# Two transformer-like layers on one core: where VectorE takes the last table doublings, the factor sums, unit 0's sum and batch 2's moments

## What is computed

```python
x = _layernorm(x + _L0_attn_ref(x, t))       # irfft(rfft(x) * rfft(t)), the first 1024 rows
x = _layernorm(x + _L0_ffn_ref(x, ...))      # shared expert + top 2 of 8 experts
x = _layernorm(x + _L1_attn_ref(x, phazor, phazor_init, last_conv_re, last_conv_im))
x = _layernorm(x + _L1_ffn_ref(x, ...))      # shared expert + top 2 of 8 experts

def _L1_attn_ref(...):
    ph = ph / mag * jnp.exp(-mag)            # one complex number per channel
    prog = ph[None, :] ** t                  # t = 0 .. 1023
    filt = prog * ph_init[None, :]
    conv = jnp.fft.ifft(filt_fft * x_fft, axis=1)[:, :L, :]
    return (conv + last_conv * prog * ph).real
```

## Time and profile before

| | us |
|---|---|
| median of 3 runs | 315.94 (315.78 to 316.88) |
| the profiled execution, whole | 315.59 |
| its span, first to last instruction | 313.8 |
| PE busy | 275.5 (88%) |
| DVE busy | 238.9 (76%) |
| ACT busy | 153.8 (49%) |
| POOL busy | 130.1 (41%) |
| mean granted TensorE clock | 0.962 of full |

### The profile page before, as it was taken

The page is one execution under the profiler, slowest core; times in us unless marked ns, Lnnn a source line. Parts: engine busy times, 40 slices in busy tenths (PEclk is TensorE's granted clock), DMA queues, the critical chain, the costliest instruction groups (busy, mean ns, idle before and its releaser), DMA issues.

```text
span 313.8 us, 3733 instructions
## 1 busy us (share of the span) xinstructions
PE 275.5 (88%) x994; PEld 157.0 (50%) x994; DVE 238.9 (76%) x563; ACT 153.8 (49%) x521; POOL 130.1 (41%) x203
## 2 busy tenths in 40 slices
PE   8699903878988599969999999999999989999993
PEld 7598803546643235425554454545445444444472
DVE  2898799795999966989698779868896863874710
ACT  0318464347722168744656467457637551632323
POOL 3668608814000122148766744874675210110112
PEclk9899985899999789999999999999999999999999
DMA  6992000008556000191009204800860293097111
GB/s 195 332 350 70 0 0 0 0 7 323 243 240 267 0 2 2 58 424 58 0 24 427 91 1 176 362 0 5 323 249 1 96 397 115 4 373 230 34 36 33
DMA packets 19269, 43.54 MB, mean 139 GB/s; under 512 B 1968, under 2 KB 14256, under 8 KB 15024
## 3 DMA queue, kind: packets, MB, share of 16 engines
q1 hardware_dynamic: 16240, 41.56, 35.5%
q10 hardware_dynamic: 2880, 1.74, 1.9%
q0 software_dynamic: 128, 0.00, 0.0%
HBM read 40.94 MB, written 2.36 MB: 138 GB/s over the span
## 4 chain that ended last, share of the span: by engine, by line
issue 30%; PE 22%; POOL 20%; DVE 19%; ACT 4%; DMA 3%; SPq 1%; POOLq 0%; ACTq 0%; DVEq 0%
PE ps L416 8%; PE ps L516 5%; DVE third L1318 4%; POOL rs L972 3%; DMA third<-in_fwd 3%; POOL second L1013 2%; POOL second L1008 2%; POOL second L1001 2%; POOL second L1009 2%; POOL rs L991 2%; POOL second L1002 2%; ACT tok L676 2%; PE ps L434 2%; POOL ve L987 1%; PE ps L513 1%
## 5 line engine op out<-in xcount | busy, mean ns | idle before, releaser
L516 PE MATMUL ps<-third,w_out 128*128 128x512 f32 x240 | 109.8, 601 | 0.0
L1318 DVE TENSOR_TENSOR third<-ps,first 128x512 f32<-128x512 f32 x120 | 73.4, 680 | 0.3
L516 PEld LDWEIGHTS ps<-third,w_out 128*128 128x128 f32 x240 | 45.0, 194 | 52.3 <-issue 44.7
L699 ACT ACTIVATE first<-ps 128x512 f32<-128x512 f32 x32 | 19.1, 597 | 22.9 <-PE ps L497 14.7
L968 POOL TENSOR_TENSOR ve<-ssq,eps 128x4 f32<-128x4 f32 x15 | 3.0, 199 | 65.4 <-ACT xy L736 51.3
L961 POOL TENSOR_TENSOR rs_<-ve_,half_neg 128x8 f32<-128x8 f32 x4 | 6.6, 1658 | 56.3 <-DVE ve_ L1236 56.3
L416 PE MATMUL ps<-second,third 128*128 128x256 f32 x96 | 24.3, 404 | 0.7 <-DVE second L1137 0.7
L1327 DVE TENSOR_TENSOR second<-ps,xT 128x512 f32<-128x512 f32 x15 | 10.2, 681 | 15.7 <-PE ps L516 15.7
L1353 DVE TENSOR_TENSOR_SCAN second<-col,second 128x512 f32<-128x512 f32 x16 | 20.8, 1337 | 1.5 <-POOL second L1001 1.5
L416 PEld LDWEIGHTS ps<-second,third 128*128 128x128 f32 x96 | 18.9, 203 | 5.7 <-issue 3.3
L1307 DVE TENSOR_TENSOR first<-ps,first 128x512 f32<-128x512 f32 x16 | 11.0, 686 | 12.8 <-PE ps L491 8.8
(11 more groups left out here) (288 smaller groups left out, 532.9 us busy)
## 6 DMA issues: line engine op xcount, KB each, us to landing
first<-gates SPq DMA_DIRECT2D x32, 1024.0 KB, 6.8
out<-xy SPq DMA_DIRECT2D x7, 256.0 KB, 4.8
third<-in_inv SPq DMA_DIRECT2D x1, 1536.0 KB, 12.6
xy<-in_L_attn_x SPq DMA_DIRECT2D x8, 128.0 KB, 8.3
xy<-in_L_attn_x ACTq DMA_DIRECT2D x8, 128.0 KB, 8.3
third<-in_fwd SPq DMA_DIRECT2D x2, 512.0 KB, 9.3
w_out<-in_L_ffn_w SPq DMA_DIRECT2D x2, 512.0 KB
third<-in_fwd ACTq DMA_DIRECT2D x1, 512.0 KB, 5.3
```

Source lines behind the costliest of these rows:

```text
L516: last_ = mm(y_ps[:], w_out[l][:, 1 + e], hs[(EXPERTS * n + e) % 16], start=False, stop=(e == EXPERTS - 1))
L699: run(sil[kind], gate_ps[:], ACT.Silu).then_inc(silu_done, 1)
L1318: tt(hs[(EXPERTS * n + e) % 16], rows[:], wbc[n % 2][:, e], MUL).then_inc(scaled, 1)
```

## The change

Four moves, and no operation is added or taken away:

- `inverse_transform(1, ...)` is cut behind its ninth late operation, and `add_input(0)` is put in the cut. It stood at the head of VectorE's slot 1.
- `moments1(2)` stood behind it, ahead of both `hidden` of slot 1, and stands behind them now.
- `table_sums(8)` and `table_sums(9)`, which stood around the late inverse sums, stand behind rows 0 and 4 of `scale_rows(2)`. ScalarE's `table_products(9)` goes from ahead of slot 0 into slot 1, behind `squares(0)`.
- `factor_sums` goes from slot 2 (behind unit 3's rows, ahead of the first scan) to slot 1 (behind unit 2's rows). ScalarE's `factor_products` goes from the end of its slot 1 to ahead of `copy_channels(1, 4)`.

```diff
@@ ScalarE, slot(n)
                 if n:
                     squares(n - 1)
+                if n == 1:
+                    table_products(9)
                 if n in TURN_SLOT:
                     normalise1(TURN_SLOT[n][0])
                 if n:
                     normalise(n - 1)
                 if n - 1 in ROUTE_SLOT:
                     copy_gates(ROUTE_SLOT[n - 1])
+                if n == 1:
+                    factor_products()
                 if n in TURN_SLOT:
                     copy_channels(1, TURN_SLOT[n][0])
                     normalise1(TURN_SLOT[n][1])
@@
                 if 0 <= n - 3 < GROUPS:
                     normalise3(n - 3)
-                if n == 1:
-                    factor_products()
@@ ScalarE, ahead of the slots
             table_products(8)
-            table_products(9)
@@ VectorE, inverse_transform, part 1
                     stt(f, p, -0.5, e, MUL, ADD).then_inc(step, 1)
+                if part == 2:
                     own("y3")
@@ VectorE, slot(n)
-                if n:
+                if n > 1:
                     add_input(n - 1)
-                if n in (1, 2):
-                    moments1(n + 1)
+                if n == 2:
+                    moments1(3)
@@
                 between = {}
+                if n == 1:
+                    moments1(2)
+                    between[0] = lambda: table_sums(8)
+                    between[4] = lambda: table_sums(9)
@@
                     scale_rows(n + 1, between)
-                if n == 2:
+                if n == 1:
                     factor_sums()
@@ VectorE, ahead of the slots
             inverse_transform(0, 1)
+            inverse_transform(0, 2)
             moments1(0)
@@
             scale_rows(1, {})
-            table_sums(8)
             inverse_transform(1, 1)
-            table_sums(9)
+            add_input(0)
+            inverse_transform(1, 2)
```

## The result

The changed kernel takes 312.81 us in the median of 4 runs (312.33 to 313.10), the kernel before 315.86 (315.10 to 316.88) on the same chip: ratio 0.9897, 95% interval 0.9869 to 0.9925. That is 3.1 us faster; 3.7 were forecast (312.2, range 311.6 to 314.4). The profiled execution is 312.82 us long, its span 311.0. Each set has its own runs of the kernel before.

A forecast was written before the change was run, and what follows sets the result against it. TensorE was taken as the bound from slot 3 on. 0.53 + 3.17 + 0.2 = 3.9 us, less 0.2 for the clock, gave 3.7: 315.59 to 311.9 profiled, median 0.35 above, 312.2 us, range 311.6 to 314.4.

The forecast's parts named there:

- What bounds the kernel: From the 18th slice (133 us), slot 3 on, TensorE is the bound, at 9 tenths in nearly every slice.
- the sum 4.8 us sooner: Slot 1: unit 0's sum starts 4.80 us sooner, but TensorE then idles 4.8 us ahead of unit 4's transposes; worth nothing itself.
- The chain through batch 2: Slot 1, batch 2's moments to unit 5's normalisation: unit 5's rows and the rest of TensorE's slot 1 come 0.53 us sooner.
- The factor sums out of the way: Slot 2: the scan starts without a wait, so TensorE's wait ahead of unit 2's tokens goes: 3.17 us, plus 0.2.
- The 0.2 for a start from idle: Unit 2's four transposes, 0.66 us, lose about 0.2 us that a start from idle adds; an estimate.
- The clock: Slot 1: half clock around TensorE's idle time costs 0 to 3.0 us, 0.2 taken; rival that it lasts: 0.14, 313.7 to 315.2.
- The table sums beside GpSimd's power: Slot 1: table sums 8 beside batch 2's power take their usual time, nothing added; rival that they wait: 0.07, 313.4 us.
- the rule of the Trainium skill: VectorE instructions with two SBUF inputs and GpSimd instructions reading SBUF exclude each other; by it table sums 8 would wait.

The follow-up runs named there:

- chain sooner: Changed kernel with factor products behind unit 5's copy, factor sums in slot 2, batch 2's moments, table sums 8 and unit 5's normalisation earlier: 309.79 us, second set 310.76.
- the other two sets: The changed kernel unaltered, run again in two more sets against the kernel before: 312.35 and 311.82 us, ratios 0.9879 and 0.9860.
- chain and start: Chain sooner plus seven matmuls of no use behind the second filter block, while TensorE waits for its matrices at the start: 309.58 us.
- chain in both slots: Chain sooner with, on ScalarE in slot 2, unit 7 normalised directly behind unit 6, both ahead of unit 6's copy: 309.11 us.
- all but the factors: Changed kernel with factor products and factor sums put back to where they stood before, the other three moves kept: 315.59 us, ratio 0.9984.

## Why the prediction was right, point by point

**What bounds the kernel**: right, with one slice misread. In the earlier trace rows the 18th slice (133 to 141 us) is at 6 tenths, since it holds the wait of 3.01 us; the nines begin behind it. After, it is at 9 too. From slot 3 on PE is at 9 tenths in both profiles, and slot 0 to end shrinks by what PE gains at unit 2's tokens, 3.74 (47.40 us behind slot 0, 51.14 before).

**Slot 1, the sum 4.8 us sooner and worth nothing in itself**: right, 4.75 us idle behind experts 4, for which 4.8 were worked out.

**The chain through batch 2, 0.53**: right to 0.04, seen at unit 5's transposes (27.44 behind slot 0 against 117.74 - 89.73 = 28.01, so 0.57). That it is so short because the factor products hold the copy was worked out too. That another order is worth more I had not seen: chain sooner gains 3.8 us on the changed kernel in a profile without a fall of the clock, 2.1 in one with a fall, and 1.1 by the medians of the set that holds both.

**The factor sums out of the way, 3.17 + 0.2**: the 3.17 are right (3.2 measured alone). The 0.2 for a start from idle was over-sized: the four transposes take 0.60 instead of 0.66, so 0.06. Together, 0.57 + 3.17 + 0.06 are the 3.8 us by which slot 0 to end shrinks.

**The clock, 0.2 taken, 3.0 as its upper end**: over-sized by 0.2: it cost nothing. It was low for 6.8 us, as long as before (105.5 to 112.36), but I had let that time run from PE's return. It ran from the fall, and that came 2.1 us ahead of PE's return (0.8 before), so it was over at 117.8, ahead of 118.19. The forecast of 3.7 lies so close to 3.8 because this term of 0.2, taken for nothing, and the 0.14 too much for the start from idle nearly cancel. That part is luck.

**The table sums beside GpSimd's power**: as read from the earlier trace rows. They start at 109.19 within the power of 108.74 to 110.40 and take 0.48 each, as ever. So the rule of the Trainium skill ("SBUF — State Buffer", section "SBUF: two separate sides") that I set against it does not show where the power starts first. It does for a plain product of 512 columns: before, the first half of the scan, beside `drive_state`'s second product, took 2.21 us, where a half alone takes 1.26. And it shows for a power that starts second: at 149.07 in the profile before, beside a half of the next scan that was under way, it took 1.87 us, where the others of its kind take 1.01.

```profile
147.45 2.69 DVE L1353 TENSOR_TENSOR_SCAN second<-col,second 128x512 f32<-128x512 f32 x2
```
```profile
149.07 1.87 POOL L991 TENSOR_TENSOR rs<-ve,half_neg 128x4 f32<-128x4 f32 x1
```

**What was left out**: the start. I set the profiled execution against its median by 0.35 us and took that as all that executions differ by; the changed kernel's own profile began 1.0 us later. The gain of the median, 3.1, is 0.6 under the forecast, and 4.0 and 4.3 in the other two sets lie above it. The profiled execution began late by 1.0 us; for the other three of its set no trace says so.

## What to carry to other kernels

When a step is moved ahead, look for the next thing its consumer waits for before counting the gain: here 4.8 us of sooner sum were worth nothing, and one late producer, pulled from the path ahead of a bound engine, was worth 3.2. Compare profiles from an event behind the start if the start differs by chance. And look behind a pause of the matmul engine before filling it: here a filler ahead of a second pause of 2.74 us made the profile 1.3 us longer, and one with none behind it left a spread of 1.0 us between executions in place of 3.5 and 2.9.

## What the runs showed of the hardware

The granted clock is a matter of chance between executions of one kernel. After 3.2 us of idle time it stayed at full in two profiles (chain sooner, chain and start) and fell in two (chain sooner's second set, chain in both slots). After 3.0 us it fell in one profile (all but the factors) and not in another (before). A fall with nothing waiting behind it cost 1.7 us in two profiles (3.4 us at half) and 3.0 in one (6.1 us at half with TensorE at work); in the changed kernel it cost nothing, since TensorE waited behind it anyway.

In slots 1 to 3 the clock fell during idle times of 2.7 to 4.8 us or up to 1.2 us behind them, and then stayed at half (1.2 GHz) for 3.4 or 6.8 us; from within the pause of 12.2 us ahead of slot 0 on it was at half for 10.2 to 13.7. One profile of a kernel with such a pause is not enough.
